# Adding the causal mask on VectorE, inside the row-maximum instruction, instead of on TensorE

## What is computed

```python
q = jnp.einsum('bsd,dhk->bshk', resid, W_Q)
k = jnp.einsum('bsd,dhk->bshk', resid, W_K)
...
scores = jnp.einsum('bqhc,bshc->bhqs', q, k) / sqrt(64)
scores = jnp.where(causal_mask, MASK_FILL, scores)    # key after query
probs = jax.nn.softmax(scores, axis=-1)
z = jnp.einsum('bhqs,bshc->bqhc', probs, v)
```

## Time and profile before

| | |
|---|---|
| median of 3 runs | 2064.4 us (2064.32 to 2065.5) |
| the profiled execution's own time | 2063.25 us |
| its span in the profile | 2061.4 us |
| TensorE matmul busy | 1850.7 us (90%), 22601 instructions |
| VectorE busy | 1419.1 us (69%), 2688 instructions |
| ScalarE busy | 1517.9 us (74%) |
| GpSimd busy | 1324.6 us (64%) |
| reductions L543 on VectorE | 1280, 724.0 us, mean 603 ns |
| mask products L734 on TensorE | 512, 112.3 us, mean 221 ns |

### The profile page before, as it was taken

The page is one execution under the profiler, slowest core; times in us unless marked ns, Lnnn a source line. Parts: engine busy times, 40 slices in busy tenths (PEclk is TensorE's granted clock), DMA queues, the critical chain, the costliest instruction groups (busy, mean ns, idle before and its releaser), DMA issues. The chain is left out here.

```text
span 2061.4 us, 54692 instructions
## 1 busy us (share of the span) xinstructions
PE 1850.7 (90%) x22601; PEld 1309.1 (64%) x22601; DVE 1419.1 (69%) x2688; ACT 1517.9 (74%) x3151; POOL 1324.6 (64%) x738
## 2 busy tenths in 40 slices
PE   3788988999999999999999999999999977989997
PEld 2455656565656565656666666666666647878886
DVE  3886868686867676767677676768685837555563
ACT  1587787888888887888887878787879873654454
POOL 2365766676867676867676768676767786342342
PEclk9899999999999999999999999999999998999998
DMA  3002010101010101010101010101000214111210
GB/s 107 17 5 68 15 42 2 42 2 43 2 42 2 43 5 40 4 40 7 38 9 36 10 35 10 35 12 33 14 31 15 91 43 168 62 62 62 84 61 21
DMA packets 48647, 75.09 MB, mean 36 GB/s; under 512 B 5904, under 2 KB 32784, under 8 KB 48144
## 3 DMA queue, kind: packets, MB, share of 16 engines
q1 hardware_dynamic: 48400, 71.59, 10.9%
HBM read 33.82 MB, written 20.97 MB: 27 GB/s over the span
## 5 line engine op out<-in xcount | busy, mean ns | idle before, releaser
L456 POOL TENSOR_TENSOR p_lo<-p_full,p_hi 128x1024 f16<-128x1024 f32 (+1 forms) x640 | 1164.0, 1842 | 509.0 <-ACT p_full L504 507.4
L503 ACT ACTIVATE p_hi<-psum 128x512 f16<-128x512 f32 (+3 forms) x1280 | 716.6, 560 | 244.5 <-PE psum L769 130.8
L543 DVE TENSOR_REDUCE row_max<-psum 128x1 f32<-128x512 f32 (+3 forms) x1280 | 724.0, 603 | 89.6 <-PE psum L731 61.6
L504 ACT ACTIVATE p_full<-psum 128x512 f32<-128x512 f32 (+3 forms) x1280 | 724.3, 568 | 0.0
L791 PE MATMUL psum<-v,p_hi 128*128 128x64 f16 x4352 | 511.1, 195 | 0.0
L789 PE MATMUL psum<-v,p_hi 128*128 128x65 f16 x4352 | 508.3, 193 | 1.8 <-POOL p_lo L456 1.8
L793 PE MATMUL psum<-v,p_lo 128*128 128x65 f16 x4352 | 506.3, 192 | 0.0
L731 PE MATMUL psum<-ka,qa 128*128 128x512 f16 (+3 forms) x1280 | 438.8, 351 | 53.9 <-DVE kb L573 23.3
L763 PE MATMUL psum<-qa,ka 128*128 128x512 f16 (+3 forms) x1280 | 444.2, 348 | 23.7 <-ACT p_full L504 18.0
L791 PEld LDWEIGHTS psum<-v,p_hi 128*128 128x128 f16 x4352 | 407.0, 97 | 72.6 <-issue 0.5
L789 PEld LDWEIGHTS psum<-v,p_hi 128*128 128x128 f16 x4352 | 410.4, 96 | 57.2 <-POOL p_lo L456 2.2
(11 more groups left out here) (126 smaller groups left out, 2968.9 us busy)
## 6 DMA issues: line engine op xcount, KB each, us to landing
zT_dram<-z_T SPq DMA_DIRECT2D x16, 1024.0 KB, 4.3
shared_z<-zT_dram SPq DMA_DIRECT2D x28, 512.0 KB, 6.6
qb<-qa SPq DMA_DIRECT2D x128, 64.0 KB, 1.9
ka<-ka SPq DMA_DIRECT2D x128, 64.0 KB, 1.9
shared_z<-xT_dram SPq DMA_DIRECT2D x8, 512.0 KB, 7.2
xs<-x_dram SPq DMA_DIRECT2D x8, 512.0 KB, 5.8
out_dram<-shared_w SPq DMA_DIRECT2D x8, 512.0 KB, 3.3
w_raw_rest<-wqkv_dram SPq DMA_DIRECT2D x1, 2304.0 KB, 14.4
```

The source lines that it names most:

```text
L456: nc.gpsimd.tensor_tensor(p_lo[:, at % NP, cols], p_full[:, at % NP, cols], p_hi[:, at % NP, cols], ALU.subtract).then_inc(probs_split, 1)
L503: nc.scalar.activation(p_hi[:, at % NP, to], lane_bank(a)[:, P * f:QB], ACT.Exp, scale=1.0 / SCORE)
L504: nc.scalar.activation(p_full[:, at % NP, to], lane_bank(a)[:, P * f:QB], ACT.Exp, scale=1.0 / SCORE).then_inc(lane_read, 1)
L543: nc.vector.reduce_max(row_max[:, n % MAXES, t, c:c + 1], bank_of(r)[:, 0:chunk_width(n, t, c)], AX.X).then_inc(ring_read, 1)
```

## The change

`mask_q` becomes 512 columns wide; its first 384 are 0 and its last 128 hold the triangle, so that the slice `mask_q[:, QB - w:QB]` is the mask of a diagonal chunk of any width w. On diagonal chunks VectorE's reduction is replaced by `tensor_tensor_reduce`: it adds the mask to the bank, writes the sum back to the bank, and takes the maximum on the way. TensorE's mask product L734 is gone; the score product now ends the bank by itself.

```diff
-        mask_q = sb("mask_q", [P, P], BF16)
+        mask_q = sb("mask_q", [P, QB], BF16)
...
-            nc.gpsimd.affine_select(out=mask_q[:, :], in_=mask_q[:, :], compare_op=ALU.is_ge, fill=NEG, base=0,
+            nc.gpsimd.affine_select(out=mask_q[:, QB - P:QB], in_=mask_q[:, QB - P:QB], compare_op=ALU.is_ge, fill=NEG, base=0,
...
-                nc.vector.reduce_max(row_max[:, n % MAXES, t, c:c + 1], bank_of(r)[:, 0:chunk_width(n, t, c)],
-                                     AX.X).then_inc(ring_read, 1)
+                w = chunk_width(n, t, c)
+                bank, most = bank_of(r)[:, 0:w], row_max[:, n % MAXES, t, c:c + 1]
+                if c == block_of(n)[1]:
+                    nc.vector.tensor_tensor_reduce(out=bank, in0=bank, in1=mask_q[:, QB - w:QB], scale=1.0, scalar=NEG,
+                                                   op0=ALU.add, op1=ALU.max, accum_out=most).then_inc(ring_read, 1)
+                else:
+                    nc.vector.reduce_max(most, bank, AX.X).then_inc(ring_read, 1)
...
-                diagonal = c == q
...
-                                        start=True, stop=not diagonal)
-                if diagonal:
-                    last = nc.tensor.matmul(bank[:, w - P:w], ident_b[:, :], mask_q[:, :], start=False, stop=True)
+                                        start=True, stop=True)
```

## The result

The changed kernel takes **2073.42 us** (median of 5 runs, 2069.85 to 2074.8) against 2064.32 (5 runs): a ratio of 1.0041, with a 95% interval from 1.0027 to 1.0056. In a second series (e3) it was 2077.04 against 2065.85, ratio 1.0049 [1.0036, 1.0063]. So the change costs 8 to 11 us.

A forecast was written before the change was run, and what follows sets the result against it. TensorE was taken as busiest, waiting for VectorE's maxima in places. VectorE's 1.16 us less TensorE's 0.66 made +0.5 us in a pair, 16 times +8 us: 2071 for the profiled execution, 2072 us as median; range 2048 to 2097.

The forecast's parts named there:

- The write-out, "I take 0.11": VectorE's second instruction per diagonal chunk, writing out the maximum: 0.11 us, between a lower end of 0.07 and 0.20.
- d: VectorE's added time per diagonal chunk, pass plus write-out: 0.12 us, between 0.08 and 0.21.
- The pass, "I take 0.01, by the nearest row": VectorE's pass over a diagonal bank: 0.01 us longer, from a 694 ns row writing SBUF against the 683 ns reduction.
- The rival built on it: VectorE's write-out is nearly free, d 0.075 to 0.08, the two terms cancel: 2060 to 2068 us; chance 0.20.
- Where it meets the path: Block-by-block count of the VectorE delays that TensorE's waits hang on: 1.16 us in a pair at d = 0.12.
- 13d - 0.4: VectorE delay reaching TensorE in a pair, summed over the eight blocks, less slack in blocks 3 and 6: 1.16 us.
- 0.66: TensorE's saving in a pair, in us: 12 of the mask products count, at 0.055 us each.
- "TensorE's waits for `neg_max` and for maxima should grow by about 1 us in a pair": Sign expected in the profile after, along with a pair about 0.5 us longer.
- The wider memset: GpSimd's wider mask fill before the first pair, while TensorE waits for data: costs nothing, at most under a microsecond.
- Rival 1: VectorE's slack takes all its added work; a pair changes by -0.5 us, kernel faster at 2056 us; chance 0.23.
- Rival 3: VectorE's write back to PSUM takes turns with the read: d 0.45, 4.8 us in a pair, 2141 us; chance 0.06.
- Rival 4: TensorE's array is so well overlapped that its mask products cost nothing now; no chance of its own given.

The follow-up runs named there:

- e3: The changed kernel, unchanged, run once more for a second profile: 2077.04 us, ratio 1.0049 to the kernel before.
- e9: The changed kernel with TensorE's mask product kept everywhere, so the mask is added twice (VectorE's part alone): 2079.74 us.
- e1: The kernel before without the mask products, VectorE's plain reduction kept, scores scaled down by 256 (TensorE's part alone): 2055.11 us, ratio 0.9946.
- e5: The changed kernel with TensorE's mask products kept as well in blocks 0 to 2: 2070.19 us, ratio 1.0025 to the kernel before.
- e7: The kernel before with the whole change made in blocks 4 and 5 only: 2065.74 us, ratio 0.9994.
- e11: The changed kernel with its sum written to SBUF and all TensorE mask products kept, mask added twice: 2072.12 us, ratio 1.0027 to the kernel before.
- e8: The changed kernel with the masked sum written to spare SBUF instead of PSUM from the second pair on: 2058.0 us, ratio 0.9965 to the kernel before.
- e12: The changed kernel with TensorE's mask products kept as well in block 0 only: 2066.76 us, ratio 1.0006 to the kernel before.
- e4: The kernel before, unchanged, run once more for a second profile: 2066.16 us.
- e10: The change with its sum written to SBUF, in blocks 3 to 7 only, the rest as in the kernel before: 2059.08 us, ratio 0.9963.

## Why the prediction came out as it did

The number was near, 2072 against 2073.42, and the sign right, but by luck. The sum behind it had an undisturbed pair 0.7 us too long, or some 11 us in all (+0.5 forecast, -0.2 measured), mainly because VectorE's price was too high (1.16 forecast, 0.6 measured in e9). A cost that the sum didn't have took its place: the falls of TensorE's clock, and a later start.

- **The write-out, "I take 0.11": this is the step that failed.** The nearest row was `neg_max`, an instruction with a wait for a semaphore and another's result in front of it. The write-out needs the result in front of it too, but the pass behind it starts at the same time; a front chunk costs (0.21 - 0.09) / 3 = 0.04 us more in all, and only the last one, whose write-out `neg_max` waits for, 0.09. d came out at 0.05, outside the range of 0.08 to 0.21, and below the 0.08 at which the prediction has its own sum change sign.
- **The pass, "I take 0.01, by the nearest row".** 713 against 683 ns is 0.03; with the sum in SBUF, which is what the nearest row had, it is 687. Writing to PSUM was the one thing that no row showed, and with what it adds to the write-out it made up 0.16 of the 0.21 us.
- **The Trainium skill's 75 ns per instruction** ("Vector Engine (DVE) Microarchitecture Reference", Measured stream behaviour on trn2) was the nearer figure, and still too high for this pair of instructions. The rival built on it, a write-out nearly free, describes an undisturbed pair best.
- **Where it meets the path.** With d = 0.05 the slack of 0.2 swallows the front maxima of blocks 3 and 6, and 13d - 0.4 becomes 7d = 0.35; less 0.66 that is -0.3 in a pair. Measured at full clock: -0.2. So with the measured d the net of the account would have held to 0.1 us, but by two errors that cancel: 1.0 saved (e1) where I had 0.66, in part because in blocks 3 and 6 an earlier TensorE does more than "only waits longer", and 0.6 paid (e9), 12 d where 7 should have been left.
- **"TensorE's waits for `neg_max` and for maxima should grow by about 1 us in a pair"**: they grew by 2.5, the weight loads' waits for the ring by 1.0 and those ahead of the turns by 1.5 (2.9 and 1.3 in the rows above, 2.1 and 0.6 before). The direction proves nothing, since the pair shrank all the same: TensorE without its masks comes earlier to the same waits. And a pair got 0.2 us shorter, not 0.5 longer, at all joins without a fall but one.
- **What made the kernel slower is in no step.** By its queues the change is worth -0.2 x 12, some -2 us over the twelve steady distances. The falls of TensorE's clock give +3 in one profile and nearly +11 in the other. I had read the clock as "granted in full over the attention" and left it at that. It goes with both idle spells at the join being long, in four combinations: 1.26 and 0.19 to 0.31 (before, e5 to e7, e9 to e11) no fall; 1.43 and 0.25 (e1, e8) none; 1.32 and 0.36 (e12) none; 1.43 and 0.36 (the change, e3) falls at 9 of 24 joins. Each of the other kernels has one profile with 12 joins, before two.
- **The wider memset** was put at nothing, "while TensorE waits for data". TensorE's first matmul hangs on it: it starts at 22.6 us in every profile with the wide mask, and at 22.3 in the three without (before, e4, e1), 0.3 us, within the microsecond that the prediction allowed.
- **Rival 1** (faster, slack takes it) was right about the direction of an undisturbed pair, with -0.5 us against the measured -0.2. **Rival 3** (read and write take turns) is out: 713 ns, not over 1 us. **Rival 4** is out by e1.

Not settled: why only some joins with the same two spells fall, and whether the change would fall on the chips of e5 to e8 and e12. Nor the differences of 1 to 7 us in the start and the first three pairs, where the clock of every kernel here changes level several times; e5 is at its mark in the fourth pair 6.0 us later than e12 (414.9 against 408.9), and I can't say why. The stretch behind the last `neg_max` varies as well, from 392.8 us (e10) to 396.7 (e1). They are part of the 8 to 11 us too: by the change's own profile 2.5 of its 6.4 us lie ahead of the first `neg_max`, where a repeat of the kernel before came 2.1 us later as well, and 1.5 in the first three pairs.

## What to carry to other kernels

Where an instruction must write an output that nobody reads, choose the memory it goes to by experiment: here SBUF instead of PSUM turned a loss of 0.4% into a gain of 0.35%. When an edit takes work from TensorE in front of a wait, look at how long its idle spells at that place become and at the granted clock behind them, in narrow windows and in more than one execution; the 40 slices of the page hid it: up to 1650 us the row PEclk reads the same in before, the change and e3. And a grown sum of waits says nothing by itself: compare the period of the loop at a fixed mark.

## What was not expected of the hardware

- On VectorE the write-out of an accumulated maximum starts together with the next pass: 0.14 us long, 0.00 apart from it (911.39, 911.77, 912.29).
- Writing the sum to PSUM instead of SBUF lengthens the pass over 512 columns from 687 to 713 ns and the write-out from 83 to 135 (means of each); the pass is nowhere near twice as long.
- The granted clock fell to 0.50 for about 3.4 us behind idle spells of only 1.43 and 0.37 us, in a pair in which TensorE is busy 94% of the time (93.95 of 100 us from 893 in the change), at some joins and not at others with the same two numbers. The Trainium skill ("TensorE: Matmul & The Clock Gate", "A second HAM failure mode: psum-queue depth-cycling") tells of another kernel in which small, frequent idle gaps between groups of matmuls were enough to swing the clock between its two levels. The windows of e3 agree in kind: 0.89, 0.50 and 0.90 behind two such gaps.
- A kernel with four more matmuls on TensorE in a pair was 7 to 10 us faster (e12 against the change and e3, on another chip).
